# A decoder layer with routed experts on one core: the third group's q and k projected inside the first group's flow, and the work of the opening dealt out anew

## The reference

```python
q = sigmoid(heads(Wq, bq)); k = sigmoid(heads(Wk, bk)); v = heads(Wv, bv)
normal = arange(L) + 1
sink_in  = normal / einsum(q + EPS, cumsum(k) + EPS)
src_out  = normal / einsum(k + EPS, cumsum(q) + EPS)
cons_sink = einsum(q + EPS, cumsum(k * src_out) + EPS) / normal
cons_src  = clip(einsum(k + EPS, cumsum(q * sink_in) + EPS) / normal, -1, 1)
src_comp = exp(cons_src) / cumsum(exp(cons_src)) * normal
kv = cumsum(k outer (v * src_comp))
x = (q * sink_in / normal) . kv * sigmoid(cons_sink)
h = layernorm(inputs + x @ Wo + bo, ln1_g, ln1_b)
y = layernorm(h + gelu(h @ W1 + b1) @ W2 + b2, ln2_g, ln2_b)
x = layernorm(inputs + y)
e = argmax(x @ router_w.T); out = layernorm(x + relu(x @ fc[e])**2 @ proj[e].T)
```

## Time and profile before

| | us |
|---|---|
| median of 3 runs | 895.41 |
| lowest, highest | 894.64, 896.0 |
| the profiled execution, its whole time | 903.71 |
| its span | 901.9 |
| PE busy | 837.7 (93%) |
| DVE busy | 587.1 (65%) |
| POOL busy | 334.0 (37%) |
| ACT busy | 259.0 (29%) |

### The profile page before, as it was taken

The page is one execution under the profiler, slowest core; times in us unless marked ns, Lnnn a source line. Parts: engine busy times, 40 slices in busy tenths (PEclk is TensorE's granted clock), DMA queues, the critical chain, the costliest instruction groups (busy, mean ns, idle before and its releaser), DMA issues.

```text
span 901.9 us, 18877 instructions
## 1 busy us (share of the span) xinstructions
PE 837.7 (93%) x6726; PEld 642.7 (71%) x6727; DVE 587.1 (65%) x1334; ACT 259.0 (29%) x473; POOL 334.0 (37%) x425
## 2 busy tenths in 40 slices
PE   7678998999999999999999798999999999999994
PEld 3366666566666666666666566688899999999994
DVE  7879677878878978978978836255434444444332
ACT  2224413424424424424424213232221122221110
POOL 8221512615814814724724614415322222222222
PEclk9679998999999999999999999998999999999998
DMA  8999993001001001000000000964555555455540
GB/s 256 289 310 320 312 305 101 1 2 48 15 11 48 18 8 48 24 1 25 24 2 25 25 1 19 376 209 152 188 167 181 169 172 179 173 179 174 186 158 0
DMA packets 69715, 110.55 MB, mean 123 GB/s; under 512 B 5261, under 2 KB 54287, under 8 KB 69648
## 3 DMA queue, kind: packets, MB, share of 16 engines
q1 hardware_dynamic: 66240, 101.17, 36.0%
q0 software_dynamic: 3408, 8.46, 2.5%
HBM read 66.94 MB, written 43.58 MB: 123 GB/s over the span
## 4 chain that ended last, share of the span: by engine, by line
PE 87%; DVE 5%; issue 3%; ACT 2%; POOL 1%; DMA 1%; POOLq 0%; DVEq 0%; SPq 0%; ACTq 0%
PE bank L802 15%; PE bank L812 14%; PE bank L729 12%; PE bank L739 11%; PE bank L527 6%; PE bank L661 5%; PE bank L628 4%; PE bank L677 4%; PE bank L533 3%; PE bank L653 2%; PE bank L760 2%; PE bank L551 2%; PE bank L543 2%; DVE cc L1210 2%; PE bank L638 1%
## 5 line engine op out<-in xcount | busy, mean ns | idle before, releaser
L802 PEld LDWEIGHTS bank<-xsT,fc 128*128 128x128 f32 x1248 | 147.9, 195 | 3.3 <-issue 1.7
L802 PE MATMUL bank<-xsT,fc 128*128 128x128 f32 x1248 | 149.0, 279 | 1.0 <-ACT xsT L962 1.0
L1079 POOL TENSOR_TENSOR rstd<-vare,minus_half 128x1 f32<-128x1 f32 x96 | 65.5, 683 | 158.7 <-DVE vare L1326 158.5
L729 PE MATMUL bank<-n1T,w1s 128*128 128x512 f32 (+1 forms) x256 | 117.4, 581 | 1.6 <-ACT n1T L937 1.6
L739 PE MATMUL bank<-w2s,hT 128*128 128x256 f32 x480 | 114.2, 382 | 0.8 <-ACT hT L943 0.8
L969 ACT ACTIVATE relu<-bank 128x512 f32<-128x512 f32 x78 | 46.6, 598 | 212.8 <-PE bank L802 209.0
L739 PEld LDWEIGHTS bank<-w2s,hT 128*128 128x128 f32 x480 | 89.2, 190 | 23.0 <-issue 10.9
L1317 DVE TENSOR_TENSOR sm<-bank,upto 128x512 f32<-128x512 f32 x128 | 79.5, 684 | 31.6 <-PE bank L628 30.4
L812 PE MATMUL bank<-pj,act 128*128 x416 | 94.2, 379 | 0.0
L812 PEld LDWEIGHTS bank<-pj,act 128*128 128x128 f32 x416 | 77.0, 190 | 9.4
L1132 POOL TENSOR_TENSOR mrstd<-mvare,minus_half 128x1 f32<-128x1 f32 x39 | 22.1, 566 | 161.0 <-DVE mvare L1490 161.0
(11 more groups left out here) (212 smaller groups left out, 1385.4 us busy)
## 6 DMA issues: line engine op xcount, KB each, us to landing
...
x<-in_x SPq DMA_DIRECT2D x8, 512.0 KB, 4.4
xT<-in_xT SPq DMA_DIRECT2D x7, 512.0 KB, 5.5
...
```

The lines of the kernel that those rows point to most:

```text
L729: last = nc.tensor.matmul(pb[:, ffn_columns(g)], w1[:, k, chunk(f)], n1T[:, k, ffn_columns(g)], start=(k == 0), stop=(k == KT - 1), skip_g ...
L802: last = nc.tensor.matmul(h_bank[n][:, chunk(f)], fc[:, s, k, chunk(4 * n + f)], xsT[:, k, :], start=(k == 0), stop=(k == KT - 1))
L1079: nc.gpsimd.tensor_tensor(rstd[:, n, c], vare[:, n, c], minus_half[:], ALU.pow)\
```

## The change

- Four new steps `e_proj` project q and k of group 2 in the opening, beside group 0's flow, through two banks that are free then (`po0`, `pb`); ACT takes their sigmoids into memory that is not yet in use (`t2` and `r3` for q, the buffer of x of group 2 for k). In period 2 `a_proj` 0 to 3 of PE and ACT fall away; v and the scans stay there. So x of group 2 can be loaded only when k of that group is scaled (`load_x` waits for `kp`).
- The first `xb` is made by DVE (`t_xb`), between the masks of chunk 0, and no longer by POOL.
- Of the first split of q, POOL makes one of its two pieces, ACT the other beside its own two.
- In the opening `t_head` and the first `t_half1` change places, the scan of k's second half goes ahead of `a_comp`, and `t_shift` goes behind `p_kt` 0.
- The products of groups 1 and 2 are made in two pieces each.
- The lists of the periods are dealt anew: on POOL `p_split` first, and `b_turn` and `p_xb` behind `d_count`; on DVE `c_sum3` 0 ahead of the scans and `d_count` behind `a_proj` 5; on PE `b_down` 0 behind `p_pairs` 0, `b_down` 2 ahead of `p_pairs` 1 and some more of that kind; on ACT several steps change places.

```diff
--- before.py
+++ after.py
...
 PE_FIRST = [
...
+    ("a_proj", 1, 4), ("e_proj", 2, 0), ("a_dots2", 0, 0), ("e_proj", 2, 1), ("a_comp", 0, 0), ("a_proj", 1, 5),
+    ("e_proj", 2, 2), ("p_share2", 0, 0), ("e_proj", 2, 3), ("p_pairs", 0, 0), ("p_kt", 0, 0), ("t_shift", 0, 0),
+    ("p_mix", 0, 0), ("p_out", 0, 0), ("a_dots1", 1, 0), ("p_pairs", 0, 1), ("p_kt", 0, 1), ("p_mix", 0, 1),
...
 PE_ORDER = [
     ("p_share2", 0), ("b_turn", 0), ("d_count", 0), ("a_proj", 0), ("a_proj", 1), ("b_turn", 1), ("a_proj", 2),
-    ("b_up", 0), ("a_proj", 3), ("a_proj", 4), ("a_proj", 5), ("b_down", 0), ("b_up", 1), ("p_pairs", 0), ("p_kt", 0),
-    ("b_down", 1), ("b_up", 2), ("p_mix", 0), ("a_dots1", 0), ("c_route", 0), ("p_out", 0), ("c_logit", 0),
-    ("b_up", 3), ("p_kt", 1), ("p_pairs", 1), ("b_down", 2), ("p_mix", 1), ("p_out", 1), ("a_share1", 0), ("b_up", 4),
-    ("b_down", 3), ("c_route", 1), ("p_pairs", 2), ("c_logit", 1), ("b_up", 5), ("b_down", 4), ("b_down", 5),
+    ("b_up", 0), ("a_proj", 3), ("a_proj", 4), ("a_proj", 5), ("b_up", 1), ("p_pairs", 0), ("b_down", 0), ("p_kt", 0),
+    ("b_up", 2), ("b_down", 1), ("p_mix", 0), ("a_dots1", 0), ("c_route", 0), ("p_out", 0), ("c_logit", 0),
+    ("b_down", 2), ("p_pairs", 1), ("p_kt", 1), ("b_up", 3), ("p_mix", 1), ("p_out", 1), ("a_share1", 0), ("b_up", 4),
+    ("c_route", 1), ("b_down", 3), ("p_pairs", 2), ("b_up", 5), ("b_down", 4), ("b_down", 5), ("c_logit", 1),
     ("p_kt", 2), ("b_up", 6), ("p_mix", 2), ("a_dots2", 0), ("p_out", 2), ("c_route", 2), ("p_pairs", 3),
     ("c_logit", 2), ("p_kt", 3), ("b_up", 7), ("p_mix", 3), ("a_comp", 0), ("p_out", 3), ("b_down", 6),
...
 DVE_FIRST = [
...
+    ("a_proj", 0, 5), ("a_dots1", 0, 0), ("t_half1", 0, 0), ("a_share1", 0, 0), ("a_scan2", 0, 0), ("a_scan2", 0, 1),
+    ("a_proj", 1, 4), ("t_head", 0, 0), ("a_dots2", 0, 0), ("a_proj", 1, 0), ("a_proj", 1, 1), ("a_comp", 0, 0),
+    ("a_proj", 1, 5), ("p_share2", 0, 0), ("a_proj", 1, 2), ("p_mask", 0, 0), ("p_mask", 0, 1), ("a_proj", 1, 3),
+    ("p_mask", 0, 2), ("t_xb", 0, 0), ("p_mask", 0, 3), ("a_prod", 1, 0), ("p_state", 0, 0), ("p_sums", 0, 0),
+    ("a_dots1", 1, 0), ("p_mask", 0, 4), ("p_mask", 0, 5), ("p_mask", 0, 6), ("p_mask", 0, 7), ("t_half1", 0, 1),
+    ("p_state", 0, 1), ("p_sums", 0, 1), ("t_b1", 0, 0), ("a_share1", 1, 0), ("a_scan2", 1, 0), ("a_scan2", 1, 1),
...
 DVE_ORDER = [
-    ("p_share2", 0), ("c_sum2", 0), ("c_sum2", 1), ("a_proj", 0), ("d_count", 0), ("a_proj", 1), ("c_sum3", 0),
-    ("a_proj", 2), ("a_proj", 3), ("a_proj", 4), ("a_proj", 5), ("a_prod", 0), ("p_mask", 0), ("p_mask", 1),
+    ("p_share2", 0), ("c_sum2", 0), ("c_sum2", 1), ("c_sum3", 0), ("a_proj", 0), ("a_proj", 1), ("a_proj", 2),
+    ("a_proj", 3), ("a_proj", 4), ("a_proj", 5), ("d_count", 0), ("a_prod", 0), ("p_mask", 0), ("p_mask", 1),
     ("p_mask", 2), ("p_mask", 3), ("c_sum2", 2), ("c_sum3", 1), ("p_state", 0), ("a_dots1", 0), ("p_sums", 0),
...
 ACT_FIRST = [
...
+    ("a_proj", 1, 2), ("a_proj", 1, 3), ("e_proj", 2, 0), ("t_exp", 0, 0), ("a_dots2", 0, 0), ("e_proj", 2, 1),
+    ("p_share2", 0, 0), ("e_proj", 2, 2), ("e_proj", 2, 3), ("p_pairs", 0, 0), ("p_mix", 0, 0), ("p_pairs", 0, 1),
...
 ACT_ORDER = [
...
+    ("b_up", 0), ("c_row", 0), ("b_up", 1), ("p_pairs", 0), ("p_mix", 0), ("b_up", 2), ("c_route", 0), ("p_pairs", 1),
+    ("p_mix", 1), ("b_up", 3), ("c_row", 1), ("b_up", 4), ("c_route", 1), ("b_up", 5), ("c_row", 2), ("p_norm", 0),
+    ("p_pairs", 2), ("b_up", 6), ("p_mix", 2), ("c_route", 2), ("p_norm", 1), ("p_pairs", 3), ("a_dots2", 0),
+    ("p_norm", 2), ("p_mix", 3), ("b_up", 7), ("c_row", 3), ("c_route", 3), ("p_norm", 3),
...
 POOL_FIRST = [
-    ("p_xb", 0, 0), ("p_split", 0, 0), ("p_mix", 0, 0), ("p_mix", 0, 1), ("p_mix", 0, 2), ("p_norm", 0, 0),
-    ("p_norm", 0, 1), ("p_norm", 0, 2), ("p_mix", 0, 3), ("p_norm", 0, 3),
+    ("p_split", 0, 0), ("p_xb", 0, 0), ("p_mix", 0, 0), ("p_norm", 0, 0), ("p_mix", 0, 1), ("p_mix", 0, 2),
+    ("p_mix", 0, 3), ("p_norm", 0, 1), ("p_norm", 0, 2), ("p_norm", 0, 3),
 ]

 POOL_ORDER = [
-    ("b_turn", 0), ("p_xb", 0), ("c_sum2", 0), ("p_split", 0), ("c_sum2", 1), ("c_sum3", 0), ("d_count", 0),
-    ("c_sum3", 1), ("c_sum2", 2), ("p_mix", 0), ("p_norm", 0), ("c_sum3", 2), ("p_mix", 1), ("p_norm", 1),
-    ("p_mix", 2), ("c_sum2", 3), ("p_norm", 2), ("c_sum3", 3), ("p_mix", 3), ("p_norm", 3),
+    ("p_split", 0), ("c_sum2", 0), ("c_sum2", 1), ("c_sum3", 0), ("d_count", 0), ("b_turn", 0), ("p_xb", 0),
+    ("c_sum2", 2), ("c_sum3", 1), ("p_mix", 0), ("c_sum3", 2), ("p_norm", 0), ("c_sum2", 3), ("p_mix", 1),
+    ("p_mix", 2), ("p_norm", 1), ("p_norm", 2), ("c_sum3", 3), ("p_mix", 3), ("p_norm", 3),
 ]

 POOL_LAST = [

...
-        def q_of(g):
-            return r2[:].rearrange("p (m c) d -> p m (c d)", m=KT) if g == 1 else qT[:]
+        def q_of(g, m):
+            if g == 1:
+                return r2[:, 2 * m:2 * m + 2].rearrange("p c d -> p (c d)")
+            if g == 2:
+                return (t2, r3)[m][:].rearrange("p c d -> p (c d)")
+            return qT[:, m]
+
+        def k_of(g, m):
+            if g == 2:
+                return x[:, 2, 2 * m:2 * m + 2].rearrange("p c d -> p (c d)")
+            return kT[:, g % 2, m]
...
+                if g == 2:
+                    ev["kp"].wait(sp, g, KT)
...
-                if n == 0 and g > 0:
+                if n == 0 and g > 0 and g != 2:
+                if g == 2 and n < 4:
+                    return

...
+                    if g == 2 and n == 4:
+                        for done in ("qp", "kp"):
+                            ev[done].wait(pe, g - 1, KT)
-                last.then_inc(S["proj"], 1)
+                last.then_inc(S["proj"], 5 if g == 2 and n == 4 else 1)
+
+            def project_ahead(g, half, n):
+                if n == 0:
+                    pe.wait_ge(xT_in[half], 16)
+                    ev["sig"].wait(pe, 1, 4)
+                elif n >= 2:
+                    ev["sig"].wait(pe, g, n - 1)
+                for k in range(KT):
+                    last = nc.tensor.matmul((po0, pb)[n % 2][:], (wk, wq)[n // 2][:, k, chunk(n % 2)], xT[:, half, k, :],
+                                            start=(k == 0), stop=(k == KT - 1))
+                last.then_inc(S["ahead"], 1)
...
-                if n < 4:
+                if n < 4 and g != 2:
-                        dst, bias = kT[:, half, m, :], bk
+                        dst, bias = k_of(g, m), bk
-                        dst, bias = q_of(g)[:, m, :], bq
+                        dst, bias = q_of(g, m), bq
+
+            def squash_ahead(g, half, n):
+                ev["ahead"].wait(act, 0, n + 1)
+                m = n % 2
+                nc.scalar.activation((k_of, q_of)[n // 2](g, m), (po0, pb)[m][:], ACT.Sigmoid,
+                                     bias=(bk, bq)[n // 2][:, m:m + 1]).then_inc(S["sig"], 1)

...
+                    if g == 0 and m == KT - 1:
+                        nc.scalar.activation(qm[:, 1, m], qs[:, m], ACT.Copy, scale=parity[:, 1:2])\
+                            .then_inc(S["qm1"], 1)

...
             def add_bo(g, half, _):
+                if g == 0:
+                    return
...
             def split_q(g, half, _):
-                for m in range(KT):
+                for m in range(KT - 1 if g == 0 else KT):
...
+            def first_xb(g, half, _):
+                dve.wait_ge(x_in[0], 16)
+                dve.wait_ge(tables_in, 16 * 9)
+                nc.vector.tensor_tensor(xb[:], x[:, 0], bo[:].unsqueeze(1).broadcast_to([P, NC, D]), ALU.add)\
+                    .then_inc(S["xb"], 1)
+

...
+                if g > 0 and g <= 2:
+                    for m in range(KT):
+                        last = nc.vector.scalar_tensor_tensor(cc[:, w, m], (q_of, k_of)[w](g, m), EPS_FLOW, cc[:, w, m],
+                                                              ALU.add, ALU.mult)
+                    last.then_inc(S[done], 1)
+                    return

...
-                    nc.vector.tensor_tensor(qs[:, m], BANK4[m][:], q_of(g)[:, m], ALU.mult).then_inc(S["qp"], 1)
+                    nc.vector.tensor_tensor(qs[:, m], BANK4[m][:], q_of(g, m), ALU.mult).then_inc(S["qp"], 1)
-                    nc.vector.tensor_tensor(kT[:, half, m], BANK4[2 + m][:], kT[:, half, m], ALU.mult)\
+                    if g == 2:
+                        ev["s"].wait(dve, 0, 4 * NC)
+                        ev["kt"].wait(dve, 0, NC)
+                    nc.vector.tensor_tensor(kT[:, half, m], BANK4[2 + m][:], k_of(g, m), ALU.mult)\

```

More of the change, by code:

```diff
@@ L56 @@
 EVENTS = {
-    "proj": 6, "sig": 4, "v": 4, "scan1": 4, "carry1": 1, "dot1": 2, "hs1": 1, "rden": 1, "cz": 1,
+    "proj": 6, "sig": 4, "v": 4, "scan1": 4, "carry1": 1, "dot1": 2, "ahead": 4, "hs1": 1, "rden": 1, "cz": 1,
     "bc1": 4, "scaled": 4, "scan2": 4, "carry2": 1, "dot2": 2, "hs2": 1, "cons": 1,
@@ L110 @@
     ("a_proj", 0, 0), ("a_proj", 0, 1), ("a_proj", 0, 2), ("a_proj", 0, 3), ("a_prod", 0, 0), ("a_proj", 0, 4),
```

(25 more changed lines are left out.)

33 lines of the change are left out of this document (10 added, 23 removed).

## The result

The changed kernel takes 904.51 us (median of 6 runs, 903.0 to 907.21) beside 895.02 for the kernel before in the same session (6 runs): ratio 1.0111, 95% interval 1.0089 to 1.0133. It is slower by 9.5 us, and the forecast of 893.0 with its range up to 899 was wrong.

The account below looks back on a forecast made before the run. PE was taken to bound the kernel, with room only in the opening, period 2 and period 8. Terms -5.0 + 1.3 + 2.8 - 1.5 = -2.4 us, from the median 895.41 to 893.0; range 884.5 to 899.

Parts of the forecast that it names:

- The opening, -5.0: Opening up to 98.36 us: edits on DVE's chain bring the second pairs forward; -5.0 us, between -4 and -6.
- steps (1) to (4): Opening, DVE's chain: shorter t_head, POOL's first xb gone, pause filled, split shared; first pairs 6.1 us earlier.
- step (3): Opening: DVE does more behind the products, PE gives back 0.9 and 1.9 us; qs begins at 40.6 instead of 44.6.
- The early projections: Opening: four e_proj, 6.9 us of PE, cost nothing while they fill PE's 5.76 us pause.
- Period 2, +1.3: Period 2: POOL's sums hold two scans, PE pauses and runs at half clock; +1.3 us, ends -4.4 and +3.
- The exclusive lock: VectorE and GpSimd share a port pair, taken whole per instruction; in period 2 each POOL sum holds a scan 2.1 us.
- Periods 4 to 7, +2.8 with ends at 0 and 8: Full periods: POOL's later sums hold DVE's products and delay the pairs; 0.7 us each, +2.8 for four.
- the other case: Periods 4 to 7: b_turn starts behind c_sum3 1, at 317.2; the pairs come 0.3 us late.
- the caught case: Periods 4 to 7: b_turn starts at 316.1, the product is held till 318.7; the pairs come 1.9 us late.
- Period 8, -1.5: Period 8: masks 1 us earlier, some of PE's 8.1 us not busy goes; -1.5 us, between +0.5 and -5.
- The slower one: Rival: xb late in each of periods 4 to 7, 1.9 to 2.2 us each; +5.0 in all, 900.4; chance 0.18.
- Nothing collides: Rival: POOL's sums slip between DVE's products, period 2 gives -4.4; -10.9 us in all, 884.5; chance 0.15.

Follow-up runs that it names:

- the second trace: Kernel before, unchanged, run again: 894.49 us, span 892.7; where the opening is judged, the changed kernel run again: 901.35 us, ratio 1.0082.
- e4: Changed kernel with only POOL's list altered, p_xb ahead of d_count and b_turn behind it: 891.37 us, ratio 0.9908; again on another chip 891.62, ratio 0.9963.
- the first: First trace of the kernel before, unchanged, from which the forecast was worked: an execution of 903.71 us.

## Why the prediction was wrong, point by point

- **What bounds the kernel.** Right, and it is what made the error dear: "work taken off another engine gains nothing, and a new wait of PE is paid in full" in the full periods.
- **The opening, -5.0.** Measured -3.1 and, in the second trace, -4.1. Counted from the shares of group 0, which came 1.45 us later than in the trace I worked from, steps (1) to (4) came within 0.5 (`qs` at 41.0, which is what the terms of step (3) add up to, where I wrote 40.6): first dots 31.7 (31.5 said), first pairs 44.0 (43.7), products of group 1 over at 52.6 (52.4). The step that failed is the last, "the second pairs start at 54.8": they start at 58.3, in e4 at 56.2. I had put `t_shift` at 3.9 us beside the masks. In the profiled execution it took 6.02, at a granted clock of 0.57, and what follows ran at 0.50 up to 58 us. Of the nine traces with this opening three have it at about 6 us and an opening of 74.6, six at 3.7 to 4.2 and 73.5. The other 1.4 us are there in e4 too, where PE comes to the dots only at 53.8, behind the mix and the output projection that stand ahead of them in its list:

```profile
46.84 6.02 PE L593 MATMUL bank<-be1c,w1s 128*128 128x1 f32 x32
...
59.75 1.15 PE L657 MATMUL bank<-qm,kT 32*128 32x256 f32 x16 [1.09 <-DVE num L1304]
```

- **The early projections.** Right: they fill the pause, 0.82 us of it is left ahead of the first dots, and the dots (1.08) and the v projection (1.97) run at full clock.
- **Period 2, +1.3.** Measured +1.2 and +0.7 against the second trace, 0.0 against the first: the number is partly luck. One scan was held and not two (3.30 us), so v was there 1.4 us earlier than I had it, and the pairs 1.0 (by my own terms v would have been at 112.7, as 108.5 and 4.2 are not 112.2). The pairs ran at half clock, as said:

```profile
104.57 3.30 DVE L1256 TENSOR_TENSOR_SCAN cc<-ones_t,r 128x512 f32<-128x512 f32 x1
```

```profile
104.42 2.37 POOL L1113 TENSOR_TENSOR x<-x,be2s 128x1024 f32<-128x1024 f32 x1
106.75 3.26 POOL L1108 TENSOR_TENSOR xb<-x,bos 128x1024 f32<-128x1024 f32 x1
```

```profile
109.65 2.09 PE L657 MATMUL bank<-qm,kT 32*128 32x256 f32 x16 [3.84 <-DVE vpad L1285]
```

- **The exclusive lock.** "SBUF — State Buffer", "SBUF: two separate sides", of the Trainium skill says that the one who starts first has the pair for the whole instruction. The length of the holds agrees, 3.27 us beside one sum. That the caught product had started first doesn't: it is recorded 0.3 to 0.6 us ahead of the sum, if POOL's starts are exact enough for that. Who gets in between two sums changed from case to case. The scans did: at 107.87 the one of the changed kernel is over, and the second sum takes 3.26 instead of 2.36. In the four full periods of the changed kernel the product didn't. In period 3 of the kernel before a product of `c_sum2` did, and the second sum took 2.54 (second trace):

```profile
162.84 1.53 DVE L1360 SCALAR_TENSOR_TENSOR t<-r,mv,g2s 128x256 f32<-128x256 f32 x1
```

```profile
161.74 2.36 POOL L1073 TENSOR_TENSOR x<-x,be2s 128x1024 f32<-128x1024 f32 x1
164.05 2.54 POOL L1068 TENSOR_TENSOR xb<-x,bos 128x1024 f32<-128x1024 f32 x1
```

- **Period 3, 0 to 0.5.** Measured +0.3 against the second trace.
- **Periods 4 to 7, +2.8 with ends at 0 and 8: this is the step.** Measured +14.1 and +12.5. The place and the time were right: `b_turn` began 23.2 us into the period, where I had 22.5 to 23.4, and I had written out the case in which "the product is held till 318.7, the sum till 321.3 and all behind it". Three things were wrong. I chose the other case by a margin of under 1 us, on the ground that the transfers would stretch; the fourth ended at 246.69, and the product that was caught began at 246.37. I priced the caught case at 1.9, with one product held by the first sum and the next by the second; one product was held by both, what follows it began only then, and PE's waits alone grew by 9.2 in four periods, 2.3 each. And I gave the wait no loss of clock, though the earlier trace rows show one after a pause and I had charged it in period 2; it is 1.6 in three of the four. So the far end of the term was 8 where it had to be 14.
- **Period 8, -1.5.** Measured -1.2, against the second trace. That the number is near is luck, as far as is known. The idle time of PE, which was to go, is 4.7 us there and 4.1 in the second trace of before; what is shorter is its busy time (51.47 against 53.33), for a reason that no run tells. "Some of the 8.1 us in which PE isn't busy" read a stall of that execution as room in the kernel; 5.6 of the 63.0 us belonged to it.
- **The rivals.** The slower one is what happened, in its place and by what was named in its favour ("DVE's order puts the sum of `c_sum3` 1 ahead of `state` and the spread"), not by its headline: `xb` itself was ready 3 us early. It cost 3.5 us a period instead of 1.9 to 2.2. At 0.18 it had too little. "Nothing collides" is what e4 comes near to in periods 4 to 7; in all it is 3.8 us shorter than the second trace of before, and the 10.9 lacked above all what period 2 still costs (+0.7 where that case had -4.4).
- **The profiled execution.** I wrote that only a part of period 8 touched the 8.3 us by which it was above the median. The stall there was 5.6, and a lower clock in period 3 (0.86 from 158 to 170 us) another 1.7 (68.50 against 66.79).
